# Dense matmul groups of a graph layer cut in halves, one group of adjacency windows between two halves; the scale's maximum spread over partitions by a matmul

## The reference

```python
def layer0(h):                      # h = relu(layernorm(x)), 1250 x 1024
    h = sigmoid(h @ wenc.T + benc)  # encoder, 1024 -> 500
    h2 = h @ conv_weight            # 500 -> 500
    agg = segment_sum(h2[src] * edge_weight[:, None], dst)
    return (agg + h @ lin_weight.T) @ wdec.T + bdec
x = x + layer0(relu(layernorm(x)))
# layer 1: relu(layernorm(x)) @ W.T + b, summed over neighbours and self loop
# with the weight deg^-1/2 of both ends; x = x + that
```

## Time and profile before

| | |
|---|---|
| runs | 454.25, 454.5, 455.05 us, median 454.5 |
| the profiled execution | 454.87 us; its span, first to last instruction, 453.1 us |
| granted TensorE clock | 0.991 of full speed over the span |
| TensorE busy | 443.9 us of 453.1 |
| VectorE, ScalarE, GpSimd busy | 301.0, 237.3, 42.3 us |
| stage with windows | from 42.49 us to about 132 us; the first `g` group begins at 88.93 us |

### The profile page before, as it was taken

The page is one execution under the profiler, slowest core; times in us unless marked ns, Lnnn a source line. Parts: engine busy times, 40 slices in busy tenths (PEclk is TensorE's granted clock), DMA queues, the critical chain, the costliest instruction groups (busy, mean ns, idle before and its releaser), DMA issues.

```text
span 453.1 us, 8833 instructions
## 1 busy us (share of the span) xinstructions
PE 443.9 (98%) x3202; PEld 333.4 (74%) x3202; DVE 301.0 (66%) x604; ACT 237.3 (52%) x452; POOL 42.3 (9%) x63
## 2 busy tenths in 40 slices
PE   6999999999999999999999999999999999999997
PEld 4999988978775465469888878888889844444454
DVE  5999896976864243864667775938462656567752
ACT  6987996657769552135144444658454622222220
POOL 2611200000000000000000000464600000000000
PEclk8899999999999999999999999999999999999999
DMA  8950958299458898034800007041848004324533
GB/s 279 315 175 5 170 94 139 71 325 320 134 163 155 263 89 300 4 122 187 314 1 1 1 0 259 21 187 41 286 187 323 4 7 178 120 93 139 162 119 106
DMA packets 48400, 66.37 MB, mean 146 GB/s; under 512 B 25794, under 2 KB 35025, under 8 KB 46821
## 3 DMA queue, kind: packets, MB, share of 16 engines
q1 hardware_dynamic: 48036, 65.39, 48.3%
q0 software_dynamic: 320, 0.39, 0.3%
HBM read 43.62 MB, written 16.77 MB: 133 GB/s over the span
## 4 chain that ended last, share of the span: by engine, by line
PE 88%; ACT 3%; DVE 3%; DMA 2%; SPq 2%; issue 1%; ACTq 0%; DVEq 0%
PE bank L1587 22%; PE bank L1588 21%; PE bank L1589 21%; PE bank L1603 19%; PE bank L1714 2%; PE bank L1732 2%; DMA h<-x 1%; PE bank L1757 1%; DMA h16T<-x 1%; SPq L735 1%; PE bank L1716 1%; ACT h0T L1027 1%; ACT h L979 1%; ACT stage L1076 0%; ACT cnt L1073 0%
## 5 line engine op out<-in xcount | busy, mean ns | idle before, releaser
L1603 PE MATMUL bank<-a,h_hi 128*128 128x256 f16 (+3 forms) x400 | 85.5, 270 | 0.0
L1603 PE MATMUL bank<-a,h_lo 128*128 128x256 f16 (+3 forms) x400 | 85.5, 270 | 0.0
L1587 PE MATMUL bank<-right,left 128*128 128x512 f16 (+1 forms) x148 | 54.4, 367 | 0.0
L1589 PE MATMUL bank<-right,left 128*128 128x512 f16 (+1 forms) x148 | 54.4, 367 | 0.0
L1588 PE MATMUL bank<-right,left 128*128 128x512 f16 (+1 forms) x148 | 54.4, 367 | 0.0
L1152 ACT CAST left<-zs 128x512 f16<-128x512 f32 x35 | 21.5, 617 | 60.3 <-PE bank L1589 60.3
L1572 DVE SCALAR_TENSOR_TENSOR x<-bank,dis_u,x 128x512 f32<-128x512 f32 (+2 forms) x37 | 26.7, 722 | 34.2 <-PE bank L1589 34.2
L1603 PEld LDWEIGHTS bank<-a,h_hi 128*128 128x128 f16 (+1 forms) x400 | 38.9, 97 | 4.1 <-issue 0.3
L1603 PEld LDWEIGHTS bank<-a,h_lo 128*128 128x128 f16 (+1 forms) x400 | 39.1, 98 | 3.8
L1587 PE MATMUL bank<-h0T,we 128*128 128x256 f32 (+3 forms) x144 | 41.3, 287 | 0.5 <-DVE h0T L1308 0.5
L1587 PE MATMUL bank<-unit,g 128*128 128x500 f16 (+3 forms) x120 | 40.8, 340 | 0.0
(11 more groups left out here) (191 smaller groups left out, 972.6 us busy)
## 6 DMA issues: line engine op xcount, KB each, us to landing
whole<-w SPq DMA_DIRECT2D x7, 1024.0 KB, 7.9
adj_scratch<-stage SPq DMA_DIRECT2D x50, 125.0 KB, 3.2
right_scratch<-right SPq DMA_DIRECT2D x5, 1024.0 KB, 4.0
right<-right_scratch SPq DMA_DIRECT2D x5, 1024.0 KB, 4.8
h<-x SPq DMA_DIRECT2D x9, 512.0 KB, 6.9
x<-x SPq DMA_DIRECT2D x9, 512.0 KB, 5.9
out<-x SPq DMA_DIRECT2D x18, 256.0 KB
w_tile<-w SPq DMA_DIRECT2D x8, 512.0 KB, 4.9
```

The source lines that it names most:

```text
L1587: pe.matmul(o, lhs[0], rhs[0], start=first, stop=False, skip_group_check=True)
L1589: return pe.matmul(o, lhs[1], rhs[0], start=False, stop=last, skip_group_check=True)
L1603: ins = pe.matmul(o, h1[i][0:n, k, 128 * f:128 * (f + 1)], moving, start=(k == 0 and part == 0 and i == 0), stop=(k == T - 1 and part == p ...
```

## The change

1. Every dense group behind `("edges",)` becomes two steps, `("half", ...)` with the first half of the k-tiles and the group itself with the second half. Both accumulate in the same bank.
2. The due time has two slopes: windows 0 to 21 (SLOW = 22) are spread over the encoder's share of the groups, the others over the rest.
3. `sizes` is spread by a matmul with the identity (the new step `("spread", "wc")`, behind `("e", 2, 3)` and window 8), and VectorE reduces the bank; the store, the load, a memset on GpSimd and their semaphores go.
4. `("limits", "scale")` and the four `("cut", "wc", k)` stand earlier in the encoder.
5. One `w1` size and load fewer stand beside the windows, one more in the aggregation's second stage; `("bounds",)` stands behind its eighth product instead of its sixth.
6. `benc` is loaded behind the second tile of x.

```diff
+SLOW = 22
...
-        (2, 3): [("norm", 9), ("split", 8), ("turn", 8), ("limits", "out")],
-        (3, 0): [("split", 9), ("turn", 9)], (3, 1): [("limits", "in")], (3, 2): both(turn(4)),
-        (4, 0): [("limits", "scale")], (4, 1): cut_wc[:1], (4, 2): cut_wc[1:3], (4, 3): cut_wc[3:],
+        (2, 3): [("norm", 9), ("split", 8), ("turn", 8), ("spread", "wc")],
+        (3, 0): [("split", 9), ("turn", 9), ("limits", "scale")], (3, 1): cut_wc[:1], (3, 2): both(turn(4)), (3, 3): cut_wc[1:2],
+        (4, 0): cut_wc[2:3], (4, 1): cut_wc[3:],
...
-    for k, s in enumerate([("g", 2), ("g", 4), ("g", 6), ("g", 8), opening[0]]):
+    for k, s in enumerate([("g", 2), ("g", 4), ("g", 6), ("g", 8)]):
...
     def due(w):
-        return w + OPEN * (NW - w) / NW
+        if w < SLOW:
+            return OPEN + (share - OPEN) * w / SLOW
+        return share + (NW - share) * (w - SLOW) / (NW - SLOW)
+
+    groups = [s[0] for s in dense[dense.index(("edges",)):] if s[0] in ("e", "g", "swl")]
+    share = NW * groups.count("e") / len(groups)
...
+    dense = dense[:begin] + [p for s in dense[begin:] for p in ([("half", *s), s] if s[0] in ("e", "g", "swl") else [s])]
...
-                spent += s[0] in ("e", "g", "swl")
+                spent += 0.5 * (s[0] in ("half", "e", "g", "swl"))
...
-            if (n, k) == (1, 5):
+            if (n, k) == (1, 7):
                 steps += [("bounds",)]
...
-            if n == 1 and k in (1, 2, 3):
-                steps += [("size", "w1", KD - 4 + k)] + [("load", "w1", KD - 2 + k)] * (k == 1)
+            if n == 1 and k in (1, 2, 3, 4):
+                steps += [("size", "w1", KD - 5 + k)] + [("load", "w1", KD - 3 + k)] * (k < 3)
...
                 if t == 1:
                     sp.dma_start(ew_raw[:], nat_w).then_inc(ew_in, 16)
+                    sp.dma_start(benc_c[:], benc).then_inc(benc_in, 16)
...
-            sp.dma_start(benc_c[:], benc).then_inc(benc_in, 16)
...
                 elif s == ("limits", "scale"):
-                    dve.wait_ge(limits_in, 16)
-                    link(v.tensor_reduce(limits[:, 0:1], all_limits, AX, ALU.max))
+                    g = ("spread", "wc")
+                    acc_done(dve, g)
+                    v.tensor_reduce(limits[:, 0:1], bank[banks_of[g]][:, 0:P], AX, ALU.max).then_inc(bank_free, 1)
+                    read_done(dve, g)
...
+                    if s == ("spread", "wc"):
+                        pe.wait_ge(sizes_ready, 1)
+                        pe.matmul(take(s)[:, 0:P], sizes[:].broadcast_to([P, P]), ident[:], start=True, stop=True,
+                                  skip_group_check=True).then_inc(acc_ready, 1)
...
-                        for k in range(KD if len(group) == 1 else 0):
+                        ks = range(KD)
+                        if halved:
+                            ks = ks[:KD // 2] if s[0] == "half" else ks[KD // 2:]
+                        for k in ks if len(group) == 1 else ():
```

More of the change, by code:

```diff
@@ L332, in build @@
             bank_for(("s", s[1], s[2]), *dense)
-        elif s[0] in ("t", "e", "g", "z"):
+        elif s[0] in ("t", "e", "g", "z") or s == ("spread", "wc"):
             if not by_dma(s):
@@ L346, in build @@
                 bank_for((*s, i), *dense)
-        if s[0] in ("t", "e", "g", "z", "s", "p", "o", "edges"):
+        if s[0] in ("t", "e", "g", "z", "s", "p", "o", "edges") or s == ("spread", "wc"):
             parts = 2 if s in HALVED else {"s": KF, "p": 2}.get(s[0])
@@ L358, in build @@
             frees[s[1:]] = len(frees)
+        elif s == ("limits", "scale"):
+            frees["spread", "wc"] = len(frees)
     nth = {(p, b): p * NB + b for p in range(NP) for b in range(NB)}
@@ L419, in build @@
         minus_half = small("minus_half", [P, 2], F32)
-        sizes = small("sizes", [P, 2], F32)
+        sizes = small("sizes", [P, 1], F32)
         ew_sizes = small("ew_sizes", [EP, 1], F32)
@@ L1736, in run @@
                             idle(IDLE[4])
-                    elif s[0] == "e":
-                        b, f = s[1:]
+                    elif s[0] in ("half", "e") and s[-3] == "e":
+                        b, f = s[-2:]
                         if b == 0 and f < PAIR:
@@ L1743, in run @@
                             group = (f,)
-                        os = [take(("e", b, g))[0:feat_rows(g), 0:block_cols(b)] for g in group]
+                        halved = ("half", "e", b, f) in STEPS
+                        os = [(bank[banks_of["e", b, g]] if s[0] == "e" and halved else take(("e", b, g)))[0:feat_rows(g), 0:block_cols(b)] for g in group]
                         if len(group) > 1:
@@ L1768, in run @@
                                     ins.then_inc(acc_ready, 1)
-                    elif s[0] == "g":
-                        t = s[1]
+                    elif s[0] in ("half", "g") and s[-2] == "g":
+                        t = s[-1]
                         n = tile_rows(t)
-                        o = take(s)[0:n, 0:F]
+                        o = (take(s[1:]) if s[0] == "half" else bank[banks_of[s]])[0:n, 0:F]
                         read_done(pe, ("e", t // 2, KF - 1))
-                        for k in range(KF):
+                        for k in range(KF // 2) if s[0] == "half" else range(KF // 2, KF):
                             cut_done(pe, "wc", k)
@@ L1778, in run @@
                                           [wc[i][0:r, k, :] for i in range(2)], k == 0, k == KF - 1)
-                        ins.then_inc(acc_ready, 1)
-                    elif s[0] == "swl":
-                        n, f = s[1:]
+                        if s[0] == "g":
+                            ins.then_inc(acc_ready, 1)
+                    elif s[0] in ("half", "swl"):
+                        n, f = s[-2:]
                         c, m = agg_cols(n), feat_rows(f)
-                        o = take(("s", n, f))[0:m, 0:c]
-                        for k in range(KF):
+                        halved = ("half", "swl", n, f) in STEPS
+                        o = (bank[banks_of["s", n, f]] if s[0] == "swl" and halved else take(("s", n, f)))[0:m, 0:c]
+                        ks = range(KF)
+                        if halved:
+                            ks = ks[:KF // 2] if s[0] == "half" else ks[KF // 2:]
+                        for k in ks:
                             cut_done(pe, "wl", k)
@@ L1789, in run @@
                                           [hT[i][0:r, k, S * n:S * n + c] for i in range(2)], k == 0, False)
-                        if f == KF - 1:
+                        if f == KF - 1 and s[0] == "swl":
                             ins.then_inc(wl_used, 1)
```

19 lines of the change are left out of this document (2 added, 17 removed).

## The result

The changed kernel took 456.51 us (median of 11 runs, 455.25 to 457.7), the kernel before 455.19 us on the same chip (11 runs, 454.25 to 455.9): ratio 1.0028, 95% interval 1.0019 to 1.0038, or **1.3 us slower**. A second comparison on another chip gave 456.04 against 455.36 us, 1.0017 [1.0007, 1.0027]. So the change costs 1.3 and 0.7 us. The forecast of 455.2 us was +0.7 us on a median of 454.5; in its 11 runs the kernel before took 455.19 us, so about half of the 1.3 us between 455.2 and 456.51 is a difference of the kernel before to its own first three runs.

The account below looks back on a forecast made before the run. TensorE's chain of waits was taken as the bound, with only its standstills to win back: -3.2 + 1.8 + 0.2 + 1.8 + 0.1 = +0.7 us on the 454.5 us median, so 455.2 us; 8-in-10 range 453.3 to 456.6.

Parts of the forecast that it names:

- same: Outcome class for the whole kernel: neither faster (below 453.6 us) nor slower (above 455.4 us); chance 0.45.
- second rival: Window stage: ScalarE's long pieces still stand before single copies, 3.2 us of gaps stay, +2.1 us, 456.6 us; chance 0.28.
- Seven gaps gone, -3.2 us: TensorE's seven standstills in the window stage (ScalarE's copies, block 4's operand, window tensors, wc cut) all vanish: -3.2 us.
- Returns, +1.8 us: TensorE: each return from a window to dense matmuls costs 0.08 us; 22 more returns, +1.8 us.
- Spread, +0.2 us: TensorE gets one 128-column full float32 product for the wc sizes, +0.2 us; its bank costs nothing.
- New gaps, +1.8 us: New TensorE waits at windows 9, 16 and 31, from queues on ScalarE and VectorE, together +1.8 us.
- (a): Window 9 waits for window 7's copies behind ScalarE's block 3 and tile 8 work: 0.4 us, between 0 and 1.
- (b): Window 16's tensors stand behind block 4's low part on VectorE: a gap of 0.9 us, between 0.3 and 1.3.
- (c): Window 31 needs window 29's copies, behind the first w1 tile on ScalarE: 0.5 us, between 0 and 1.8.
- three windows moved out of the encoder: Encoder: 3 x 0.365 us of windows are moved, not saved; the wc cuts move ahead of g0, ending their 0.57 us.
- benc, +0.1 us: Kernel start: the load goes ahead of x's third tile, its issue hidden; between 0 and 0.84, taken as +0.1 us.
- first rival: Window stage: even dealing works, the foreseen new gaps don't open, -1.1 us, 453.4 us; chance 0.24.

Follow-up runs that it names:

- benc back: The changed kernel with benc's load back behind all early loads, all else as changed: 455.46 us (1.0016), and 455.42 us (1.0007) when run again.
- the kernel with whole groups, even, in the new places: The kernel before with spread, scale, wc cuts, w1 sizes and bounds moved as in the change; uncut dense groups, old due times: 453.53 us (0.9958), again 453.23 us (0.9957).
- the kernel with whole groups and the missing k-tiles: Uncut dense groups with steps moved as in the change, but k-tiles 0 and 1 of the conv_weight product left out: 455.44 us, 1.0005 against the kernel before.
- the other kernel: The kernel before with only the wc maximum spread by a matmul, also leaving out k-tiles 0 and 1 of the conv_weight product: 452.79 us, 0.9952.
- the whole groups with the slope: The changed kernel with uncut dense groups and benc's load at its old place, two-slope due times kept: 456.92 us, 1.0037 against the kernel before.

## Why the prediction was right or wrong

The range (453.3 to 456.6) held the time. The likeliest case, "same" at 0.45, was missed by the first comparison (0.28% over the kernel before) and met by the second (0.17%). As a time, 456.51 us is the 456.6 of the second rival, "the gaps only move", at 0.28, and its 3.2 us of new gaps are what the first profile shows. But part of that agreement is luck. The rival asks for +2.1 us on 454.5; against the kernel that ran beside it the change cost 1.3 and 0.7 us, which is inside the forecast's own range of -0.5 to +1.3. The gaps also vary: 3.2 and 2.6 us in the two profiles of the changed kernel, 2.0 and 1.7 with benc back. The rival decides from 2.0 us of new gaps, and over that both profiles of the changed kernel are. The forecast's terms, one by one:

- *Seven gaps gone, -3.2 us*: right. With halves all seven are gone. What the prediction didn't ask is which part of the change removes them: the kernel with whole groups, even, in the new places has lost the gaps for h0T, window 19's o_key and wc too, and the halves add no gain to that. The step "with one window per half group the demand is even" was granted without a price, and failed: ScalarE's long pieces are not cut, and gaps of 1.15 us stayed in the halved kernel with even due times.
- *Returns, +1.8 us*: right. 0.19 us against 0.12 at 41.73, and 2.0 us for 25 returns between two kernels that differ by the halves alone. The Trainium skill (TensorE: Matmul & The Clock Gate, "Step-by-step: what each phase is for") lets weight loads run ahead of matmuls; the trace shows that this doesn't make a change from short fp16 matmuls back to dense ones free. What holds the second start back isn't shown.
- *Spread, +0.2 us*: right, 0.23. That its bank costs nothing is right as well, but only because the scale step moves with it; at the scale's old place the bank cost 0.88 and 1.34 us. The prediction counted the banks in rotation and not how long this one is held.
- *New gaps, +1.8 us*: the step that failed. they were put at 1.8 us and measured 3.2. (a) at window 9 was 0.4 and measured 0.74 us: tile 8's first pass began at 57.58, only 0.1 us sooner than before (0.5 with the later front taken off) where 0.7 was foreseen. (b) at window 16 was 0.9 and measured 0.66, (c) at window 31 was 0.5 and measured 0.89. Their places are as named, and their sum of 2.3 us is within the bounds; in the other profile of the same kernel (b) was absent. In (b) the start of block 4's low part, 72.5 foreseen and 72.89 measured, is right by luck: the transposes were to be issued 1.5 us sooner and were not, but took 1.4 us less from issue to ScalarE's first copy. What is missing is the fourth, 0.92 us at window 36. The walk in step order was made up to the first w1 tile and stopped there; carried on by five windows it would have met the second tile's sum, now with a cut of wl and window 36's tensors queued behind it. The part "three windows moved out of the encoder" was costed as moved, not saved, and it is there that the cost arose.
- *0.5 us at the end of the stage*, won with every halved kernel (0.03 us between the two starts instead of 0.53): not predicted. It was not among the seven gaps of before.
- *benc, +0.1 us*: not settled; between nothing (455.31 against 455.21 us) and 0.6 us (456.04 against 455.42), within the bounds. That the issue would be hidden is wrong: it puts off the issue of the third tile's load by 0.38 us.
- *Later stages, 0*: right. Behind the last window both profiles take 320.7 us.

With the measured terms, the front's 0.4 us among them: -3.2 - 0.5 + 1.8 + 0.2 + 3.2 + 0.4 = +1.9 us, where the two profiled spans differ by 2.1. The medians differ by 1.3 and 0.7 us, and gap (b) isn't there in every execution.

The first rival, "the even dealing works", would have needed the new gaps to stay away. That the small moved steps alone, without halves, took 453.53 and 453.23 us where that rival had 453.4 is chance: that kernel keeps 1.16 us of gaps and pays for no further return.

## What to carry to other kernels

Cutting work finer for an even demand pays only if the waits come from bursts of the demand. Here, with even due times, they came from long pieces on the supplying engine, and each cut cost 0.08 us of TensorE for certain; only where the slope had put three windows together did the cuts win more than they cost. Moving short work from one stretch to another shifts its order against everything that stays in the list, so walk each in-order queue to the end of the stretch, not to the first close call. And test the parts of a bundle apart: a bundle that lost 1 us held a part that wins 2.

## What the runs showed of the hardware

**The clock.** In the kernel with whole groups and the missing k-tiles, TensorE stood 4.2 us from 97.92 to 102.14 us, and after it the matmuls of 500 columns started 0.42 us apart instead of 0.23. The timeline of TensorE:

```profile
102.14 0.27 PE L1712 MATMUL bank<-o_key,o_src 128*128 128x100 f16 x1 [4.03 <-ACT stage L1068]
...
103.33 0.62 PE L1582 MATMUL bank<-wc,hT 128*128 128x500 f32 x1
103.75 0.62 PE L1583 MATMUL bank<-wc,hT 128*128 128x500 f32 x1
```

and its busy time and granted clock by stretches (columns: us of the stretch, busy, clock, DMA share, GB/s):

```profile
95.00:98.00 3.00, 1.08 (x21) 1.00 1.01 403
102.00:106.00 4.00, 3.86 (x27) 0.52 0.90 240
```

The clock fell to its lower level (0.52 of 2.4 GHz is about 1.2) for some 3 us. The same came behind gaps of 3.11 and 2.25 us there and behind one of 3.20 us in the other kernel (granted clock 0.50 in the microseconds behind them); behind the gaps of 1.96 us there, 1.91 in the other kernel and 1.89 in the whole groups with the slope, and behind all shorter ones, the matmuls kept their distance. So each of those four gaps cost more than its length; the largest gap of the change is 0.97 us.

**A branch hidden.** The 0.5 us of "issue" behind the last window, where the program reads a flag and branches, is there in all eight profiles in which the last two windows come as a pair, and in none of the six in which a half group stands between them. Why a single one hides it isn't shown.

**A load's landing.** The first w1 tile was issued within 0.12 us of the same time in two runs and used 1.5 us apart, in a stretch where the DMA engines are full (their busy share from 93 to 101 us reads 1.0 in both); over all profiles it is 6.5 to 8.5 us. From these traces a wait for such a load can't be predicted to better than that.
